# VectorE does the first shared job right behind the slots and the block lists in pieces; TensorE's waits ahead of the blocks stand at their first use

## The chip, the cores and the metric

One core of one Trainium2 chip runs the whole program. The metric is the device time of one execution in microseconds (us). A span is the same execution as the profiler sees it, from the first to the last instruction. The engines are TensorE (PE), VectorE (DVE), ScalarE (ACT), GpSimd (POOL) and SyncE (SP, which here issues the loads and stores).

## The reference, cut to what matters

The program is a transformer layer on x of 2 x 1024 tokens by 256 values: an attention with a bias and a mask, a second attention, then a mixture of experts and a block that is applied to the best three quarters of the tokens. The change lies in the mixture of experts:

```
logits = (x @ wt.T + logits_g) / 2 ; scores = softmax(logits)   # 8 experts
topk_w, topk_idx = top_k(scores, 2) ; topk_w normalized
y_all[e] = (leaky(x @ w_gate[e]) * (x @ w_up[e])) @ w_down[e]   # e = 0..7
y = sum over the 2 chosen experts of topk_w * y_all
p = leaky(x @ sw_gate) * (x @ sw_up) @ sw_down                  # the shared expert, 256 wide
y = y + p
scores = y @ w_router ; top_idx = top_k(scores, 768 of 1024)
out = y, but gelu(y @ w_block) at top_idx
```

## The kernel before, in words

The tokens lie in 16 tiles of 128, in four chunks of 512 (NC_ = 4). Both the shared expert and the eight routed experts are computed in full float32.

**Routing.** VectorE computes the top two experts of each token and gives each of the 4096 (token, expert) pairs a row, a slot, of the array XS in device memory, so that the pairs of one expert lie together, padded to blocks of 128 rows. There are NBK = 39 blocks. The slots are in SI; its write (L2727) raises s_route to SLOT_IDS.

**Scatter in.** From then on POOL scatters the token tiles into XS, 32 indirect DMAs of one tile each (L2380 for the first choice, L2389 for the second), in the order chunk 0 and 1 first choice, 0 and 1 second, 2 and 3 first, 2 and 3 second.

**Block lists.** VectorE orders the 39 blocks by which can be complete after how many token tiles: three waves with 8, 12 and 16 tiles scattered, which hold READY = 9, 17 and 39 blocks in all. table(w) writes for each block of wave w its expert (EBI) and its first row in XS (STI), some 15 tiny VectorE instructions on one partition, and raises s_route to TABLE[w]. SP reads STI[b] into a register and loads block b of XS into the ring XB of six buffers; the loads of a wave wait for TABLE[w] and for its scatters (s_first, s_second). TensorE reads EBI[b] into a register (read_experts), with which it addresses the expert's weights.

**Shared jobs.** The shared expert is cut into 8 jobs (4 chunks x 2 halves of 128 hidden values). gate_up(n) is 4 matmuls of TensorE into psG and psU, leaky_product(n) is 3 VectorE instructions on 128x512 that make HH (L2776, L2777, L2780), down(n) is 4 matmuls into psY (L2437), and after each two jobs shared_result(c) copies psY to Y (L2784). psG, psU and HH have two buffers each. gate_up(0) and gate_up(1) are issued before the slots are known. NF = 6 jobs (0 to 5) are done ahead of the blocks, two behind them. Eight column_product(n) (L2787) are put between the jobs: each writes one more column of the down weights WD, which the last matmul of a block reads.

**Blocks.** TensorE's loop over i does, in this order: turned(i) (transposes block i, L2495), wide(i-1) (gate and up matmuls of block i-1, L2505), turned_back(i-2) (L2515), narrow(i-3) (down matmul, L2523). ScalarE copies between them in the order XT(i) (L2619), HT(i-2) (L2626), YB(i-3) (L2632). VectorE makes a copy of the indices IB (L2811), the three instructions of the product of block b (L2819, L2821, L2825) and, for the first twelve blocks, one score_product (L2791). POOL scatters each block's result YB to YS (L2406). XB and YB are the two halves of the array XY, six buffers each: YB(b) for b of 6 and more waits until the whole trio (b-6)//3 of results has landed in YS.

**The order at the change.** Every engine executes its instructions in the order in which they are issued. Before the change VectorE does, behind the slots: the counts of whole blocks, table(0), the weights of the choices (R1, W2), need and cnt, then job 0. table(1) and table(2) follow jobs 2 and 4. TensorE waits for TABLE[0] ahead of down(1), reads up to 17 experts while the shared jobs run, and ahead of the first block waits for all six products, for y_done 3 (the third shared_result) and for all eight column products.

The functions and the loops, with their line numbers:

Of the kernel before, what the change touches and what calls it, by code (L numbers as in the profile page):

```python
# [22 lines left out]
E, M = 8, 128  # L23
# [65 lines left out]
def program(nc, x, bias1, cond, mask, g_in, null_bias, wq1, wkv1, wo1, g_out, wq2T, bq2, wk2T, bk2, wv2T,  # L89
            bv2, gamma, wtT, wgT, w_gate, w_up, w_down, sw_gate, sw_up, sw_down, w_router, w_block, out):  # L90
    top = ExitStack()
    with top:
# [2064 lines left out]
        with ExitStack() as s3:  # L2157
# [6 lines left out]
            with ExitStack() as st:  # L2164
# [246 lines left out]
                def _(pe):  # L2411
# [69 lines left out]
                    for n in range(NF):  # L2481
                        if n >= 1 and n + 1 < NF:
                            gate_up(n + 1)
                        if n == 1:
                            pe.wait_ge(s_route, TABLE[0])
                        read_experts(min(5 * n, READY[0]) if n < 4 else READY[1])
                        down(n)
# [40 lines left out]
                    pe.wait_ge(hh_done, NF)  # L2528
                    pe.wait_ge(y_done, NC_ - 1)
                    pe.wait_ge(s_side, SIDE_COLUMN)  # L2530
                    for i in range(NBK + 3):
                        read_experts(max(READY[1], i + 5))
                        if i < NBK:
                            turned(i)
                        if 1 <= i <= NBK:
                            wide(i - 1)
                        if 2 <= i <= NBK + 1:
                            turned_back(i - 2)
                        if i >= 3:
                            narrow(i - 3)  # L2540
# [123 lines left out]
                def _(dve):  # L2664
# [62 lines left out]
                    dve.tensor_copy(SI[:, :, :], SF[:, :, :]).then_inc(s_route, 1)  # L2727
                    for w in range(2):
                        chain(dve.tensor_tensor(CMP[0:1, :, :], early_n[:, w, :].unsqueeze(2).broadcast_to([1, E, NT]),
                                                fill_f[0:1, :].unsqueeze(1).broadcast_to([1, E, NT]), ALU.is_gt), True)  # L2730
                        chain(dve.tensor_reduce(whole[:, w, :], CMP[0:1, :, :], AX_X, ALU.add), True)
                    chain(dve.tensor_copy(whole[:, 2, :], nbk[0:1, :]))
                    chain(dve.memset(given[:, :], 0.0), True)

                    def table(w):
                        lo = READY[w - 1] if w else 0
                        m = READY[w] - lo
                        new = slice(lo, lo + m)
                        chain(dve.tensor_tensor(waiting[:, :], whole[:, w, :], given[:, :], ALU.subtract), True)
                        chain(dve.tensor_tensor(BEF[0:1, :, :], tri[0:1, :, :], waiting[:, :].unsqueeze(1).broadcast_to([1, E, E]),  # L2740
                                                ALU.mult), True)
                        chain(dve.tensor_reduce(ahead[:, :], BEF[0:1, :, :], AX_X, ALU.add), True)
                        chain(dve.tensor_tensor(shift[:, :], bof[0:1, :], ahead[:, :], ALU.subtract))
                        chain(dve.tensor_tensor(step[:, :], ahead[:, :], waiting[:, :], ALU.add), True)
                        chain(dve.tensor_tensor(shift[:, :], shift[:, :], given[:, :], ALU.add))
                        chain(dve.tensor_tensor(EBC[:, 0:m, :], step[:, :].unsqueeze(1).broadcast_to([1, m, E]),
                                                blk_f[:, 0:m].unsqueeze(2).broadcast_to([1, m, E]), ALU.is_le), True)
                        chain(dve.tensor_reduce(EBF[:, 0:m], EBC[:, 0:m, :], AX_X, ALU.add))
                        chain(dve.tensor_tensor(step[:, 0:E - 1], shift[:, 1:E], shift[:, 0:E - 1], ALU.subtract), True)
                        chain(dve.tensor_scalar(EBI[:, new], EBF[:, 0:m], float(E - 1), None, ALU.min))  # L2750
                        chain(dve.tensor_tensor(EBC[:, 0:m, 0:E - 1], EBC[:, 0:m, 0:E - 1],
                                                step[:, 0:E - 1].unsqueeze(1).broadcast_to([1, m, E - 1]), ALU.mult), True)
                        chain(dve.tensor_reduce(STF[:, 0:m], EBC[:, 0:m, 0:E - 1], AX_X, ALU.add), True)
                        chain(dve.scalar_tensor_tensor(out=STF[:, 0:m], in0=STF[:, 0:m], scalar=shift[:, 0:1], in1=blk_f[:, 0:m],
                                                       op0=ALU.add, op1=ALU.add), True)
                        dve.tensor_scalar(STI[:, new], STF[:, 0:m], float(P), None, ALU.mult).then_inc(s_route, 1)
# [6 lines left out]
                    table(0)  # L2763
                    chain(dve.scalar_tensor_tensor(out=R1[:, :], in0=top_s[:, 0, :], scalar=1e-20, in1=top_s[:, 1, :],
                                                   op0=ALU.add, op1=ALU.add), True)
                    chain(dve.reciprocal(R1[:, :], R1[:, :]), True)
                    for k in range(2):
                        chain(dve.tensor_tensor(W2[:, k, :], top_s[:, k, :], R1[:, :], ALU.mult))

                    dve.wait_ge(s_wb, 32)  # L2770
                    chain(dve.tensor_copy(need[:, :], need_i[:, :]))
                    chain(dve.memset(cnt[:, :, :], 0.0), True)

# [19 lines left out]

                    for n in range(NF + 1):
                        if n < NF:
                            leaky_product(n)
                            column_product(n)
                        if n >= NS_ and n % NS_ == 0:
                            shared_result(n // NS_ - 1)
                        if n in (2, 4):  # L2800
                            table(n // 2)
                    for n in range(NF, E):
                        column_product(n)
                    dve.wait_ge(y_done, NC_ - 1)
                    dve.wait_ge(s_side, SIDE_COLUMN)
                    for b in range(NBK + 1):
                        if 1 <= b <= NT - TT:
                            score_product(b - 1)
# [125 lines left out]
```

## Time and profile before

| | us |
|---|---|
| median of 3 runs | 380.38 (377.99 to 381.49) |
| profiled execution: its own time | 377.98 |
| profiled execution: span | 376.1 |
| TensorE busy / weight loads | 309.6 / 214.1 |
| VectorE busy | 220.5 |
| ScalarE busy | 136.1 |
| POOL busy | 151.3 |

The mean granted clock of TensorE over the span is 0.90 of full speed. The stretch of the change runs from 210.8 us, when the slots are known, over the shared jobs (218.5 to 246.4 us) and the 39 blocks (248.6 to 317.6 us); the end phase (two shared jobs, combination, second top-k, block) follows until 376.1 us. TensorE is busy over 80% of the span, but the shares are averages over stages: what a stage waits for is read from its timeline.

### The profile page before, as it was taken

To read this page: it belongs to the slowest core of one execution; us is meant where nothing else is said; L and a number is where in the kernel's file an instruction comes from. 1 tells how busy PE (TensorE), PEld (TensorE's weight loads), DVE (VectorE), ACT (ScalarE), POOL (GpSimd) and SP (SyncE) were. 2 spreads that over 40 slices of the span, in tenths; PEclk is the share of its full clock that TensorE was granted. 3 is DMA by queue.
4 is the path that set the end of the run, shared out by engine and by line. 5 is a ranking of instruction groups with operands and counts; after the bars stand their busy time and mean duration, and the time that the engine had idled before them with its cause. 6 is when DMAs were issued, how large, how long until landed. Compare 5 with 4: busy or idle time off the path is not lost. (4 is left out here: it accounts for less than half of the span.)

```text
span 376.1 us, 6114 instructions
## 1 busy us (share of the span) xinstructions
PE 309.6 (82%) x1659; PEld 214.1 (57%) x1659; DVE 220.5 (59%) x851; ACT 136.1 (36%) x428; POOL 151.3 (40%) x244
## 2 busy tenths in 40 slices
PE   7799999979988879768388179879999999864970
PEld 6366676546764644344174145458877786553850
DVE  4564445333632746366245758848655553699996
ACT  1365767552010741626021000015555554034420
POOL 1349989770030004161500377774565556000000
PEclk9999999999999975568769779989999999969895
DMA  5969920000059400000010032645555431660014
GB/s 153 292 139 323 298 93 3 2 1 2 0 179 264 105 0 0 2 0 0 7 46 1 34 107 99 182 127 147 161 160 164 127 105 44 208 240 3 2 59 164
DMA packets 36074, 38.01 MB, mean 101 GB/s; under 512 B 5182, under 2 KB 31679, under 8 KB 36034
## 3 DMA queue, kind: packets, MB, share of 16 engines
q1 hardware_dynamic: 31650, 29.04, 28.4%
q0 software_dynamic: 3408, 8.43, 6.1%
q8 instruction: 16, 0.26, 0.3%
q14 instruction: 24, 0.20, 0.2%
q10 hardware_dynamic: 976, 0.08, 0.2%
HBM read 21.88 MB, written 16.57 MB: 102 GB/s over the span
## 5 line engine op out<-in xcount | busy, mean ns | idle before, releaser
L2406 POOL DMA_INDIRECT YS<-XY,IB x39 | 38.4, 985 | 28.3 <-DVE IB L2811 17.1
L2505 PE MATMUL psU<-WGU,XT 128*128 x156 | 42.3, 395 | 0.1
L2619 ACT COPY XT<-psG 128x256 f32<-128x256 f32 x39 | 14.7, 377 | 51.0 <-PE psG L2495 50.7
L1193 POOL TENSOR_SCALAR UU<-UU,rs 128x257 f32<-128x257 f32 x32 | 29.9, 935 | 0.0
L2505 PEld LDWEIGHTS psU<-WGU,XT 128*128 128x128 f32 x156 | 27.3, 195 | 3.5 <-issue 0.7
L1360 ACT ACTIVATE UU<-UU,nm 128x129 f32<-128x129 f32 x64 | 28.4, 452 | 0.7 <-DVE nm L1469 0.7
L1469 DVE CUSTOM_DVE_ANT_0 UU<-psS,BI 128x129 f32<-128x129 f32 x64 | 19.1, 356 | 14.3 <-PE psS L1248 14.3
L2437 PE MATMUL psY<-SD,HH 128*128 128x256 f32 x64 | 16.9, 410 | 12.7 <-DVE HH L2780 12.7
L2380 POOL DMA_INDIRECT XS<-AI,SI x16 | 16.0, 1002 | 26.6 <-DVE SI L2727 22.0
L2819 DVE TENSOR_SCALAR LK<-psU 128x128 f32<-128x128 f32 x39 | 11.4, 291 | 24.3 <-PE psU L2505 24.3
L1192 POOL TENSOR_SCALAR UU<-UU,rs 128x129 f32<-128x129 f32 x32 | 19.7, 615 | 13.5 <-DVE rs L1479 13.4
L2523 PE MATMUL psY<-WD,HT 128*128 x78 | 23.5, 384 | 0.0
L2437 PEld LDWEIGHTS psY<-SD,HH 128*128 128x128 f32 x64 | 13.0, 207 | 17.5 <-issue 12.8
L870 POOL TENSOR_TENSOR AI<-X,CB 128x256 f32<-128x256 f32 x12 | 8.3, 723 | 35.5 <-DVE CB L1015 35.5
L1487 DVE COPY PT<-psTt 128x384 f32<-128x384 f32 x16 | 8.9, 556 | 20.3 <-PE psTt L1319 20.3
L707 PE MATMUL psS<-KE,QE 4*128 4x256 f32 x64 | 11.9, 501 | 8.6 <-DVE nm L929 8.6
L2626 ACT COPY HT<-psY 128x128 f32<-128x128 f32 x39 | 10.4, 267 | 23.2 <-PE psY L2515 23.2
L2389 POOL DMA_INDIRECT XS<-AI,SI x16 | 16.0, 997 | 4.8 <-issue 3.7
L2495 PE MATMUL psG<-ident,XY 128*128 128x128 f32 x78 | 15.6, 286 | 2.4 <-DVE WD L2787 2.2
L2632 ACT COPY XY<-psY 128x257 f32<-128x257 f32 x39 | 14.6, 374 | 6.8 <-PE psY L2523 6.3
L1002 DVE COPY PT<-psTt 128x512 f32<-128x512 f32 x16 | 10.9, 690 | 10.1 <-PE psTt L746 10.0
L2576 PE MATMUL psU<-WB,FT 128*128 128x256 f32 x64 | 15.4, 393 | 1.7 <-ACT X L2648 0.9
(342 smaller groups left out, 722.6 us busy)
## 6 DMA issues: line engine op xcount, KB each, us to landing
XS<-PZ SPq DMA_DIRECT2D x1, 5011.5 KB, 20.7
XY<-XS SPq DMA_DIRECT2D x39, 128.5 KB, 2.5
YR<-YS SPq DMA_DIRECT2D x2, 1028.0 KB, 6.8
BI<-in_bias SPq DMA_DIRECT2D x4, 512.0 KB, 8.8
X<-in_x SPq DMA_DIRECT2D x2, 768.0 KB, 10.1
out_dram<-X SPq DMA_DIRECT2D x3, 512.0 KB, 3.0
WGU<-YS SPq DMA_DIRECT2D x1, 1028.0 KB, 10.3
XY<-YS SPq DMA_DIRECT2D x1, 1028.0 KB, 12.4
```

What stands on the lines that cost most here:

```text
L1192: pool.tensor_scalar(U[:, he, 0:W1], U[:, he, 0:W1], rs[:, d, 2 * he:2 * he + 1], None, ALU.mult)
L1193: pool.tensor_scalar(U[:, he, W1:WU], U[:, he, W1:WU], rs[:, d, 2 * he + 1:2 * he + 2], None, ALU.mult).then_inc(n_done, 1)
L1360: act.activation(U[:, he, cols], U[:, he, cols], ACT.Exp, scale=-1.0, bias=nm[:, d, n:n + 1], accum_out=rs[:, d, n:n + 1]).then_inc(exp_do ...
L1469: dve.tensor_tensor_reduce(out=U[:, he, cols], in0=psS[2 * (d % 2) + he][:, cols], in1=BI[:, h, cols], scale=-1.0, scalar=-NEG, op0=ALU.ad ...
L2380: pool.indirect_dma_start(XS[:, :], bass.IndirectOffsetOnAxis(ap=SI[:, 0, t:t + 1], axis=0), AI[:, t, :], None).then_inc(s_first[c], 16)
L2389: pool.indirect_dma_start(XS[:, :], bass.IndirectOffsetOnAxis(ap=SI[:, 1, t:t + 1], axis=0), AI[:, t, :], None).then_inc(s_second[(0, 0, 1 ...
L2406: pool.indirect_dma_start(YS[:, :], bass.IndirectOffsetOnAxis(ap=IB[:, b, n:n + 1], axis=0), YB[i][:, n, :], None, bounds_check=2 * NTOK - ...
L2437: mm = pe.matmul(psY[c % 2][:, t, :], HH[n % 2][:, t * P:(t + 1) * P], SD[:, m, :], start=m == 0 and t % 2 == 0, stop=m == NS_ - 1, skip_g ...
L2495: mm = pe.transpose(psG[b % 2][:, (k * SUB + n) * P:(k * SUB + n + 1) * P], XB[b % RING][:, n, k * P:(k + 1) * P], ident[:, :])
L2505: mm = pe.matmul(psU[b % 2][:, n * D:(n + 1) * D], XT[b % 2][:, k, n * P:(n + 1) * P], WGU[:, k, bass.ds(which[b], 1), :].rearrange("p a m ...
L2523: mm = pe.matmul(result(b)[:, 0:D + 1], HT[b % 2][:, n * P:(n + 1) * P], WD[:, bass.ds(which[b], 1), :].rearrange("p a d -> p (a d)"), sta ...
L2576: mm = pe.matmul(psU[t % 2][:, 0:D], FT[:, k, t * P:(t + 1) * P], WB[:, k, :], start=k == 0, stop=k == KD - 1)
```

## The change

Nothing is computed in another way; instructions change place on VectorE, and three waits and the reads of experts change place on TensorE. SP, POOL and ScalarE are untouched.

- VectorE: leaky_product(0) comes right behind the slots. The counts of whole blocks and table(0), now cut into table_counts, table_experts and table_rows, follow around job 1. table(1) and table(2) are cut in the same way and put between the jobs; table_rows(2) is done inside the block loop at b = 2, and the weights of the choices with need and cnt at b = 3. The wait for s_wb stands ahead of the first column product.
- TensorE: the wait for TABLE[0] stands ahead of down(2), in place of down(1). Experts are read two at a time from n = 3 on, six before the blocks, and one in each turn of the block loop. The waits for y_done 3 and for the column products stand ahead of narrow(0) (i = 3), in place of ahead of turned(0).

```
                     for n in range(NF):
                         if n >= 1 and n + 1 < NF:
                             gate_up(n + 1)
-                        if n == 1:
+                        if n == 2:
                             pe.wait_ge(s_route, TABLE[0])
-                        read_experts(min(5 * n, READY[0]) if n < 4 else READY[1])
+                        read_experts(max(0, 2 * n - 4))
                         down(n)
...
                     pe.wait_ge(hh_done, NF)
-                    pe.wait_ge(y_done, NC_ - 1)
-                    pe.wait_ge(s_side, SIDE_COLUMN)
                     for i in range(NBK + 3):
-                        read_experts(max(READY[1], i + 5))
+                        read_experts(i + 6)
                         if i < NBK:
                             turned(i)
                         if 1 <= i <= NBK:
                             wide(i - 1)
                         if 2 <= i <= NBK + 1:
                             turned_back(i - 2)
+                        if i == 3:
+                            pe.wait_ge(y_done, NC_ - 1)
+                            pe.wait_ge(s_side, SIDE_COLUMN)
                         if i >= 3:
                             narrow(i - 3)
...
-                    for n in range(NF + 1):
-                        if n < NF:
-                            leaky_product(n)
-                            column_product(n)
-                        if n >= NS_ and n % NS_ == 0:
-                            shared_result(n // NS_ - 1)
-                        if n in (2, 4):
-                            table(n // 2)
-                    for n in range(NF, E):
-                        column_product(n)
+                    leaky_product(0)
+                    whole_blocks()
+                    table_counts(0)
+                    leaky_product(1)
+                    table_experts(0)
+                    table_rows(0)
+                    dve.wait_ge(s_wb, 32)
+                    column_product(0)
+                    column_product(1)
+                    leaky_product(2)
+                    column_product(2)
+                    shared_result(0)
+                    table_counts(1)
+                    leaky_product(3)
+                    column_product(3)
+                    table_experts(1)
+                    table_rows(1)
+                    leaky_product(4)
+                    column_product(4)
+                    shared_result(1)
+                    table_counts(2)
+                    leaky_product(5)
+                    column_product(5)
+                    table_experts(2)
+                    column_product(6)
+                    column_product(7)
+                    shared_result(2)
                     dve.wait_ge(y_done, NC_ - 1)
                     dve.wait_ge(s_side, SIDE_COLUMN)
                     for b in range(NBK + 1):
+                        if b == 2:
+                            table_rows(2)
+                        if b == 3:
+                            choice_weights()
                         if 1 <= b <= NT - TT:
                             score_product(b - 1)
```

whole_blocks holds the six instructions at L2729 to L2733, table_counts those at L2739 to L2745, table_experts L2746 to L2750, table_rows L2751 to L2761. At the ends of table_counts and table_experts a wait for the engine's own last result is added; choice_weights holds L2764 to L2772.

## Rows read from the trace of the kernel before

**Rows 1.** Chain that ended last (start, length, what), first and last block.

```profile
247.97 0.34 DVE X L2787
...
248.57 0.91 PE psG L2495 x4
...
319.50 2.06 DMA YS<-XY,IB
```

**Rows 2.** Timeline of VectorE, slots to job 0 (start, length, line, operation).

```profile
210.75 0.27 DVE L2729 TENSOR_TENSOR CMP<-early_n,fill_f 1x128 f32<-1x128 f32 x1
...
213.24 0.21 DVE L2746 TENSOR_TENSOR EBC<-step,blk_f 1x72 f32<-1x72 f32 x1
...
215.28 0.18 DVE L2764 SCALAR_TENSOR_TENSOR R<-top_s 128x16 f32<-128x16 f32 x1
...
216.22 0.69 DVE L2776 TENSOR_SCALAR SA<-psG 128x512 f32<-128x512 f32 x1
```

**Rows 3.** Timeline of TensorE, the shared jobs ahead of the blocks.

```profile
218.51 3.43 PE L2437 MATMUL psY<-SD,HH 128*128 128x256 f32 x8 [10.35 <-DVE HH L2780]
...
240.69 1.89 PE L2437 MATMUL psY<-SD,HH 128*128 128x256 f32 x8
244.37 1.99 PE L2437 MATMUL psY<-SD,HH 128*128 128x256 f32 x8 [1.80 <-DVE HH L2780]
```

**Rows 4.** Timeline of VectorE, table(2), job 5 and the third shared result.

```profile
240.30 0.32 DVE L2746 TENSOR_TENSOR EBC<-step,blk_f 1x176 f32<-1x176 f32 x1
...
241.17 0.30 DVE L2751 TENSOR_TENSOR EBC<-EBC,step 1x154 f32<-1x154 f32 x1
...
242.20 0.67 DVE L2776 TENSOR_SCALAR SA<-psG 128x512 f32<-128x512 f32 x1
...
246.41 1.23 DVE L2784 COPY Y<-psY 128x1024 f32<-128x1024 f32 x1 [1.75 <-PE psY L2437]
```

**Rows 5.** Timeline of POOL, last scatter into XS and first scatters of results.

```profile
252.62 1.20 POOL L2389 DMA_INDIRECT XS<-AI,SI  x1 [0.30 <-issue]
256.49 1.00 POOL L2406 DMA_INDIRECT YS<-XY,IB  x1 [2.67 <-DVE IB L2811]
257.80 1.00 POOL L2406 DMA_INDIRECT YS<-XY,IB  x1 [0.30 <-issue]
```

**Rows 6.** Landing of the scatters at L2389, then of the loads at L2339.

```profile
DMA to landing us min/median/max: 2.6/3.1/3.5
...
DMA to landing us min/median/max: 2.2/2.5/4.6
```

**Rows 7.** Timeline of SP: the loads of the blocks begin.

```profile
235.32 26.43 SPq L2339 DMA_DIRECT2D XY<-XS  x14
```

**Rows 8.** Chain that ended last: wide(10), wide(12) and wide(34).

```profile
266.52 0.87 PE psU L2505 x4
...
269.82 0.97 PE psU L2505 x4
...
307.88 0.87 PE psU L2505 x4
```

**Rows 9.** Timeline of ScalarE: YB(6), then XT(10).

```profile
264.71 0.37 ACT L2632 COPY XY<-psY 128x257 f32<-128x257 f32 x1 [0.17 <-PE psY L2523]
264.98 0.38 ACT L2619 COPY XT<-psG 128x256 f32<-128x256 f32 x1
```

**Rows 10.** Timeline of VectorE: the product of block 4 begins.

```profile
257.65 0.29 DVE L2819 TENSOR_SCALAR LK<-psU 128x128 f32<-128x128 f32 x1 [0.28 <-PE psU L2505]
```

**Rows 11.** Windows: us, busy PE, PEld, DVE, ACT, POOL, clock, DMA, GB/s.

```profile
208.20:218.50 10.30, 0.00 (x0) 0.02 (x1) 9.28 (x42) 0.00 (x0) 5.16 (x6) 0.65 0.14 51
...
246.40:248.60 2.20, 0.03 (x1) 0.06 (x2) 2.10 (x7) 0.00 (x0) 1.61 (x3) 1.00 0.23 80
...
249.60:251.70 2.10, 2.10 (x6) 1.62 (x7) 0.00 (x0) 0.29 (x1) 1.49 (x3) 0.50 0.44 134
```

**Rows 12.** Windows of TensorE alone: us, busy, granted clock, DMA share, GB/s.

```profile
144.00:146.00 2.00, 2.00 (x12) 0.50 0.00 0
```

More of the change, by code:

```diff
@@ L2727, in _, with whole_blocks, size, table_counts @@
                     dve.tensor_copy(SI[:, :, :], SF[:, :, :]).then_inc(s_route, 1)
[L2728 to L2738, printed above, removed]
+                    def whole_blocks():
+                        for w in range(2):
+                            chain(dve.tensor_tensor(CMP[0:1, :, :], early_n[:, w, :].unsqueeze(2).broadcast_to([1, E, NT]),
+                                                    fill_f[0:1, :].unsqueeze(1).broadcast_to([1, E, NT]), ALU.is_gt), True)
+                            chain(dve.tensor_reduce(whole[:, w, :], CMP[0:1, :, :], AX_X, ALU.add), True)
+                        chain(dve.tensor_copy(whole[:, 2, :], nbk[0:1, :]))
+                        chain(dve.memset(given[:, :], 0.0), True)
+                    def size(w):
+                        return READY[w] - (READY[w - 1] if w else 0)
+                    def table_counts(w):
                         chain(dve.tensor_tensor(waiting[:, :], whole[:, w, :], given[:, :], ALU.subtract), True)
@@ L2744, in table, with table_experts @@
                         chain(dve.tensor_tensor(step[:, :], ahead[:, :], waiting[:, :], ALU.add), True)
-                        chain(dve.tensor_tensor(shift[:, :], shift[:, :], given[:, :], ALU.add))
+                        chain(dve.tensor_tensor(shift[:, :], shift[:, :], given[:, :], ALU.add), True)
+                    def table_experts(w):
+                        m = size(w)
                         chain(dve.tensor_tensor(EBC[:, 0:m, :], step[:, :].unsqueeze(1).broadcast_to([1, m, E]),
@@ L2749, in table, with table_rows @@
                         chain(dve.tensor_tensor(step[:, 0:E - 1], shift[:, 1:E], shift[:, 0:E - 1], ALU.subtract), True)
-                        chain(dve.tensor_scalar(EBI[:, new], EBF[:, 0:m], float(E - 1), None, ALU.min))
+                        chain(dve.tensor_scalar(EBI[:, READY[w] - m:READY[w]], EBF[:, 0:m], float(E - 1), None, ALU.min), True)
+                    def table_rows(w):
+                        m = size(w)
                         chain(dve.tensor_tensor(EBC[:, 0:m, 0:E - 1], EBC[:, 0:m, 0:E - 1],
@@ L2755, in table @@
                                                        op0=ALU.add, op1=ALU.add), True)
-                        dve.tensor_scalar(STI[:, new], STF[:, 0:m], float(P), None, ALU.mult).then_inc(s_route, 1)
+                        dve.tensor_scalar(STI[:, READY[w] - m:READY[w]], STF[:, 0:m], float(P), None, ALU.mult).then_inc(s_route, 1)
                         if w < 2:
@@ L2761, in table, with choice_weights @@
                             chain(dve.tensor_tensor(given[:, :], given[:, :], ahead[:, :], ALU.add), True)
[L2763 to L2772, printed above, removed]
+                    def choice_weights():
+                        chain(dve.scalar_tensor_tensor(out=R1[:, :], in0=top_s[:, 0, :], scalar=1e-20, in1=top_s[:, 1, :],
+                                                       op0=ALU.add, op1=ALU.add), True)
+                        chain(dve.reciprocal(R1[:, :], R1[:, :]), True)
+                        for k in range(2):
+                            chain(dve.tensor_tensor(W2[:, k, :], top_s[:, k, :], R1[:, :], ALU.mult))
+                        chain(dve.tensor_copy(need[:, :], need_i[:, :]))
+                        chain(dve.memset(cnt[:, :, :], 0.0), True)
                     def leaky_product(n):
```

## The prediction, made before the changed kernel ran

> **What bounds the kernel now.** I read the chain of waits first. Its last unbroken part begins at 247.97 us with a column product of VectorE, which releases the first transposes of TensorE at 248.57; from there it is TensorE's work of the 39 blocks, and behind the last block a scatter, a load and VectorE's combination [rows 1]. So the time is set by when the blocks begin, by how fast they follow each other, and by a tail that the change does not touch. The next view is TensorE's timeline ahead of the blocks: it is idle for 10.35 us, until down(0) at 218.51, and its release is VectorE's HH [rows 3]. VectorE's timeline says why. The slots are out and its next instruction starts at 210.75; then come block counts and list (to 215.28) and the weights of the choices (to 216.22), and only then job 0, whose matmuls had long been issued [rows 2]. From 218.51 to 240.85 (gate_up(5) ends 0.16 after down(4) is let in at 240.69, an overlap as modelled) TensorE works without a gap, so in that stretch it is the bound [rows 3]. At the end it is VectorE again: job 5 starts at 242.20, behind table(2) (240.30 and on), and holds down(5) until 244.37 [rows 3, 4]. The third shared result (246.41, 1.23 us) and two column products then hold the first block [rows 1, 4].
>
> **What the change does, step by step.**
>
> Job 0 first. From the start of its first instruction to down(0) it takes 218.51 - 216.22 = 2.29 us [rows 2, 3]. Started at 210.75, down(0) starts at 213.04, 5.5 us earlier. The slots themselves are not moved, so POOL's scatters start and end as before. The clock does not come into it twice: down(0) took 3.43 us against 1.89 for down(4), half speed behind the idle stretch, whose mean granted clock was 0.65 [rows 3, 11]. I leave it so after the idle of 5 us.
>
> The lists in pieces. Between job 0 and job 2 VectorE has counts (210.75 to 213.24, 2.5 us), job 1 (2.1), the experts and rows (213.24 to 215.28, 2.0) and two column products (0.34 each [rows 1]): from 212.8 this ends at 220.1. Two added waits for its own results cost some 0.1 each. gate_up(2) ends at 213.0 + 3.4 + 3.4 = 219.9, so VectorE is late by 0.3 us, and that is hidden, since down(2) stands behind gate_up(3) in TensorE's queue. After this, each pair of jobs gives VectorE 2 x 2.1 of products, 2 x 0.34, one shared result of 1.14 (246.41 to the column product that follows) and one list of 3.1 at most, 9.1 us against the 10.3 us of TensorE for two gate_ups and two downs (3.43 and 1.7 each). So TensorE stays the bound and gate_up(5) ends at 213.04 + 22.34 = 235.4, with 22.34 = 240.85 - 218.51 [rows 3]. The wait for TABLE[0] ahead of down(2) costs nothing: the list is there at 219.0, down(2) comes at 225. It is also the wait behind which down(1) does not queue any more.
>
> Job 5. Its list is cut: table_counts(2) fits ahead, the rest comes behind. The product starts at 235.4 rather than 242.20, another 1.4 us, and down(5) runs from 237.5 to 239.2. Sum so far 5.5 + 1.4 = 6.9 us.
>
> The waits. turned(0) needs block 0 in XB: SP's loads start at 235.32 and take 2.5 us (2.2 to 4.6) [rows 6, 7], so 237.8, up to 239.9. It starts at about 239.2, against 248.57: 9.3 us earlier. This is the place to be careful, since VectorE is not there yet. After job 5 (237.45) it has a column product (0.34), table_experts(2) (0.87), two column products (0.68), and the shared result from 239.4 to 240.5. Then the copy of indices, one score product (0.4) and the product of block 0, three instructions of 0.29, until 242.1. Block 1 queues behind table_rows(2), 242.20 - 241.17 = 1.03 us, block 2 behind the weights of the choices, 216.22 - 215.28 = 0.94 [rows 2, 4]. With these, the products of blocks 1 and 2 end at 244.6 and 246.9, TensorE waits for both, and wide(5) starts at about 249.4. Before, it was at 266.52 - 5 x 1.65 = 258.3, with 1.65 from wide(10) to wide(12) [rows 8]. VectorE, which in steady state waits 0.28 us per block [rows 10], has caught up. So blocks stand 8.9 us earlier here. The two late jobs cost 2.0 us of a possible 10.9.
>
> The reads of experts. wide(12) to wide(34), in whose turns a read stands, is 38.06 / 22 = 1.73 us per block against 1.65 [rows 8], so 0.08 per read, called 0.1. Twelve turns get a read that they had not, one loses it. Five of them lie between wide(5) and wide(10), which is then wanted at 249.4 + 5 x 1.73 = 258.1.
>
> **What is late next: the ring of results.** POOL is in order. Its last scatter into XS starts at 252.62 whatever VectorE does; that is 1.20 + 0.30 us, and the first result can start at 254.1, in place of 256.49, where it was waiting. At a pitch of 1.31 the third result starts at 256.7 [rows 5]. YB(6) needs all three landed. The trace shows no landing for these; the scatters into XS, of the same size and engine and beside the same loads, took 3.1 us (2.6 to 3.5) [rows 6], and the last scatter of all, with nothing beside it, 2.06 [rows 1]. I take 3.1, the row of the same conditions: 259.85. ScalarE, which wanted YB(6) at about 256.5, copies it then, and XT(10) stands behind it in its queue, 0.27 after the start of YB(6) and 0.38 long [rows 9]. wide(10) therefore starts at about 260.7, not at 258.1: a stall of 2.6 us on TensorE. Before, it was 266.52. The gain is 5.8 us; two further reads and one that goes take 0.1. Later trios are safe: POOL needs 1.31 per block, TensorE 1.65 to 1.73. Sum 5.7, rounded down to 5.6.
>
> The ends of this term. Landing at 2.06 gives 6.7, at 3.5 gives 5.2. Where POOL's start behind its waits costs more than 0.30 (up to the 2.67 - 1.2 that it idled before; 1 us taken as the end), 4.2. The data of the second wave (block 9) are the last scatters but five, so near 247, plus 3.5 and 2.5 to 4.6: 253 to 255; needed at 254.7 and covered by the stall. The rule of the Trainium skill, page "DMA: Bandwidth & Descriptors", section on the anatomy of one DMA (2.0 us plus the bytes by 436 GB/s) would give an estimate of 2.3 us for a 128 KB scatter and a gain of 6.5; the scatter rows of this trace are above it, and I keep them.
>
> The tail, 317.6 us on, moves as a whole: its waits are for the blocks, not for anything absolute. So a span of 370.5, and a time of 377.98 - 5.6 = 372.4 for the profiled execution. That one was the fastest of those shown; against the median of 380.38 it is **374.8**.
>
> **The rivals.**
>
> B, the clock. TensorE stalls 2.6 us at wide(10). Behind an idle of 2.2 us (and one of 1.80 shortly before) its clock was at half, the 1.2 GHz level, from 249.6 to 251.7 at least. The price is what down(0) paid, 3.43 us for matmuls that take 1.7 at full clock [rows 3, 11]. If it falls here: gain 3.9, 376.5. Against it: in the idle stretch of 10.30 us the mean of 0.65 means that full clock was granted for 3.1 us of idleness, more than 2.6, and there is unbroken work ahead of this stall. The page "TensorE: Matmul & The Clock Gate" of the Trainium skill, section on the clock gate, says that half rate is the default, which activity lifts and idleness restores; the trace agrees in kind. Earlier drops, in 239 to 249, are covered by the ring.
>
> C, small gains. The ring with the slow ends (4.2) and the clock together (1.7) leave 2.5 us, 377.9, which is no difference by the bound below. For it: several queues now overlap that did not. Against: each end is the far one.
>
> D, slower. The clock falls at the stall and does not come back while the blocks run: at 144 us TensorE was busy 2.00 of 2.00 us at 0.50 [rows 12]. A block whose work is all TensorE's then takes 1.65 us more. It decides from 11 us of low clock on (5.6 / 0.5); 16 us cost 8.0, and the time is 382.8. Against: behind the idle of 10.35 us only down(0) was slow [rows 3].
>
> **Chances.** Forecast 0.60, B 0.22, C 0.11, D 0.07. About 1% (3.8 us) is what a measurement of this kernel can tell from no change. Faster by more: the forecast and half of B (its 3.9 lies on the bound), 0.71, called 0.72. Within: the other half of B and C, 0.22. Slower 0.06. The range: at the low end the gain of 6.7 from the lowest run of 377.99, so 371.3; at the high end B with the 1.1 us by which the highest run lies above the median, 377.6, and a part of C. 371.5 to 378.0.
>
> **What would show it.** Right: down(0) near 213.0; down(5) ending near 239.2; turned(0) without a wait for VectorE; idle TensorE of about 1 us each at blocks 1 and 2; one stall at wide(10) with ScalarE's YB(6) waiting for a DMA; POOL's first result at 254.1 with no idle before it; no stall behind block 10. Wrong: no wait at YB(6) (then the gain is nearer 8), gaps at turned(9) (loads are the bound), a clock of 0.5 behind 260, or gaps ahead of the gate_ups (VectorE is the bound of the jobs).

## The result, and the profile after

| | before | after |
|---|---|---|
| median, us | 380.38 (17 runs, 374.07 to 382.73) | 373.16 (17 runs, 369.9 to 376.65) |
| ratio | | 0.9852, 95% interval 0.9819 to 0.9885 |
| profiled execution: own time / span | 377.98 / 376.1 | 373.7 / 371.9 |
| slots known (start of the write of SI) | 210.66 | 213.00 |
| from there to the end of the span | 165.44 | 158.90 |

The ratio compares only the runs of each kernel within 1.5% of its fastest, the medians are of all its runs. By the ratio the change makes the kernel faster by 5.6 us (4.4 to 6.9; 0.0148 of 380.38), and 5.6 was predicted. That the two agree to the tenth is chance: the two medians differ by 7.2 us, and the two traces, as counted below, by 6.5. The median of 373.16 lies in the range of 371.5 to 378.0.

The two spans differ by 4.2 us only. The reading of the traces begins with why: the slots come 2.34 us later in the execution after, and nothing ahead of them was changed. Over all traces of this case they come between 208.75 (e9) and 214.24 (e5). So the stretch that the change can act on is measured from the slots, and there the gain is 165.44 - 158.90 = **6.5 us**. All times called "behind the slots" are counted so. What the scatter of the earlier part does to the timed ratio stays inside its interval.

The chain of waits that ended last, answering to [rows 1] (start, length, what):

```profile
241.10 1.99 PE psY L2437 x8
243.09 0.23 PE psG L2495 x2
...
245.68 0.29 DVE HH L2852
245.97 0.22 DVE EBC L2759
...
247.98 0.30 DVE HH L2852
...
262.04 0.37 ACT XT L2620
...
262.54 1.13 PE psU L2505 x4
...
315.54 2.06 DMA YS<-XY,IB
```

It now goes from down(5) into the first block without VectorE in between. From 245.03 to 248.33 it then runs over VectorE, which it did not before: the product of block 0, table_rows(2) (EBC and on), the product of block 1. Further on it has a new step, ScalarE's XT ahead of a block. The last scatter starts 102.54 behind the slots, 6.3 us earlier than before.

TensorE after, answering to [rows 3]: start, duration, line, operation, shapes, and the idle time before with its releaser.

```profile
215.37 3.75 PE L2437 MATMUL psY<-SD,HH 128*128 128x256 f32 x8 [4.87 <-DVE HH L2786]
218.92 2.67 PE L2426 MATMUL psG<-FT,SG 128*128 128x512 f32 x4
221.43 1.88 PE L2426 MATMUL psU<-FT,SU 128*128 128x512 f32 x4
...
238.62 1.89 PE L2437 MATMUL psY<-SD,HH 128*128 128x256 f32 x8
241.10 1.99 PE L2437 MATMUL psY<-SD,HH 128*128 128x256 f32 x8 [0.58 <-DVE HH L2786]
242.93 0.60 PE L2495 MATMUL psG<-ident,XY 128*128 128x128 f32 x4
```

down(0) comes 2.37 us behind the slots, in place of 7.85; its idle time is 4.87 in place of 10.35. It is still slow (3.75), and so is the first half of the gate_up behind it (2.67, where the next takes 1.88). down(5) waits 0.58 in place of 1.80, and the first transposes stand directly behind it: the 2.21 us for VectorE's WD are gone.

VectorE after, answering to [rows 2, 4]:

```profile
213.00 0.18 DVE L2728 CAST SI<-SF 128x32 int32<-128x32 f32 x1
213.09 0.68 DVE L2782 TENSOR_SCALAR SA<-psG 128x512 f32<-128x512 f32 x1
...
238.90 0.69 DVE L2782 TENSOR_SCALAR SA<-psG 128x512 f32<-128x512 f32 x1 [0.54 <-PE psU L2426]
...
243.13 1.23 DVE L2790 COPY Y<-psY 128x1024 f32<-128x1024 f32 x1
...
245.88 0.30 DVE L2759 TENSOR_TENSOR EBC<-EBC,step 1x154 f32<-1x154 f32 x1
...
248.19 0.17 DVE L2772 SCALAR_TENSOR_TENSOR R<-top_s 128x16 f32<-128x16 f32 x1
```

Job 0 follows the slots, job 5 waits for its matmuls and for nothing of VectorE's own, and the late pieces stand between the products of blocks 0, 1 and 2.

TensorE in the first blocks, where VectorE and the reads of experts are late. ("issue" names no releaser; ahead of 246.77 TensorE's queue is at the read of L2479, a load of EBI and register work, from 246.01 to 246.61.)

```profile
246.77 0.41 PE L2495 MATMUL psG<-ident,XY 128*128 128x128 f32 x2 [0.42 <-issue]
...
248.33 0.33 PE L2515 MATMUL psY<-ident,HH 128*128 128x128 f32 x1 [0.20 <-DVE HH L2852]
...
251.52 0.41 PE L2495 MATMUL psG<-ident,XY 128*128 128x128 f32 x2 [0.24 <-issue]
```

Then the ring of results. POOL first, answering to [rows 5], and ScalarE and TensorE, answering to [rows 8, 9]:

```profile
254.60 0.96 POOL L2389 DMA_INDIRECT XS<-AI,SI  x1 [0.30 <-DVE IB L2838]
255.87 1.00 POOL L2406 DMA_INDIRECT YS<-XY,IB  x1 [0.30 <-ACT XY L2633]
257.17 1.00 POOL L2406 DMA_INDIRECT YS<-XY,IB  x1 [0.30 <-issue]
258.47 0.98 POOL L2406 DMA_INDIRECT YS<-XY,IB  x1 [0.30 <-issue]
```

```profile
261.76 0.37 ACT L2633 COPY XY<-psY 128x257 f32<-128x257 f32 x1 [1.64 <-DMA YS<-XY,IB]
262.03 0.38 ACT L2620 COPY XT<-psG 128x256 f32<-128x256 f32 x1
```

```profile
260.30 1.03 PE L2505 MATMUL psU<-WGU,XT 128*128 x4
262.54 1.13 PE L2505 MATMUL psU<-WGU,XT 128*128 x4 [0.42 <-ACT XT L2620]
```

POOL goes from its last scatter into XS to the results with no idle but the usual 0.30. The third result starts at 258.47; ScalarE's YB(6) is let go by its landing at 261.76, 3.3 us later; XT(10) stands behind it, and wide(10) behind that, 2.24 us after wide(9) in place of the usual 1.7. This wait did not exist before.

The granted clock (windows: stretch, length, busy time of PE, PEld, DVE, ACT, POOL, clock, DMA share, GB/s), answering to [rows 11]:

```profile
213.20:216.00 2.80, 0.63 (x2) 0.57 (x3) 2.66 (x6) 0.00 (x0) 1.54 (x2) 0.59 0.04 13
216.00:220.00 4.00, 4.00 (x10) 2.86 (x9) 3.63 (x14) 0.00 (x0) 3.09 (x4) 0.50 0.35 120
220.00:240.00 20.00, 20.00 (x62) 11.59 (x62) 16.61 (x57) 0.00 (x0) 15.21 (x18) 0.99 0.33 107
...
262.00:315.00 53.00, 51.90 (x268) 40.51 (x267) 28.05 (x120) 28.43 (x93) 32.44 (x34) 1.00 0.46 131
```

Half speed (the 1.2 GHz level) up to about 220.5, since the granted clock is 0.75 in 220 to 221; full speed afterwards, across the wait at wide(10) and all blocks behind it.

One table for all executions whose signals came in time (what that means stands under "late signals" below), in us behind the slots ("product of block 38" is its last instruction):

```
                      before  after   e6      e11     e12
down(0)                 7.85   2.37    2.38    2.37    2.37
  its duration          3.43   3.75    3.75    1.97    3.75
job 5 starts           31.54  25.90   25.79   23.72   27.36
down(5)                33.71  28.10   27.98   25.92   29.53
turned(0)              37.91  29.93   29.82   27.75   35.17
wide(5)                47.55  40.47   40.29   37.89   45.07
wide(10)               55.70  49.54   48.99   46.45   53.22
product of block 38   105.07  98.76   97.91   95.92  101.95
end                   165.44 158.90  157.92  156.73  162.01
```

### The profile page after: what moved, and what is told of

Read it like the earlier page. It is cut to its first block and busy times, and to the rows that moved or that the text cites. A ratio compares the mean times of both kernels' runs of the same rounds, so it can differ in the third digit from the quotient of the medians.

```text
span 371.9 us, 6118 instructions
## 1 busy us (share of the span) xinstructions
PE 313.3 (84%) x1659; PEld 213.6 (57%) x1659; DVE 221.0 (59%) x851; ACT 135.9 (37%) x428; POOL 150.7 (41%) x244
## 5 line engine op out<-in xcount | busy, mean ns | idle before, releaser
L1487 DVE COPY PT<-psTt 128x384 f32<-128x384 f32 x16 | 8.9, 556 | 20.3 <-PE psTt L1319 20.3
L2577 PE MATMUL psU<-WB,FT 128*128 128x256 f32 x64 | 17.0, 423 | 1.7 <-ACT X L2649 0.9
L2389 POOL DMA_INDIRECT XS<-AI,SI x16 | 15.7, 982 | 4.8 <-issue 3.4
## 6 DMA issues: line engine op xcount, KB each, us to landing
XS<-PZ SPq DMA_DIRECT2D x1, 5011.5 KB, 20.7
WGU<-YS SPq DMA_DIRECT2D x1, 1028.0 KB, 10.2
```

The source lines that it names most:

```text
L2577: mm = pe.matmul(psU[t % 2][:, 0:D], FT[:, k, t * P:(t + 1) * P], WB[:, k, :], start=k == 0, stop=k == KD - 1)
```

## The experiments

**Two halves and a quarter of the change** (e1, e2, e3), and the change with the reads of experts ahead of the blocks (e4). e1 is the kernel after with TensorE's part undone, e2 the kernel before with TensorE's part done. e1's edit:

```diff
-                        if n == 2:
+                        if n == 1:
                             pe.wait_ge(s_route, TABLE[0])
-                        read_experts(max(0, 2 * n - 4))
+                        read_experts(min(5 * n, READY[0]) if n < 4 else READY[1])
...
                     pe.wait_ge(hh_done, NF)
+                    pe.wait_ge(y_done, NC_ - 1)
+                    pe.wait_ge(s_side, SIDE_COLUMN)
                     for i in range(NBK + 3):
-                        read_experts(i + 6)
+                        read_experts(max(READY[1], i + 5))
...
-                        if i == 3:
-                            pe.wait_ge(y_done, NC_ - 1)
-                            pe.wait_ge(s_side, SIDE_COLUMN)
```

e3 is the kernel before with one move, to right behind the write of SI (the definition of leaky_product moves with it):

```diff
+                    leaky_product(0)
...
                         if n < NF:
-                            leaky_product(n)
+                            if n:
+                                leaky_product(n)
```

e4 is the kernel after with the reads taken early:

```diff
-                        read_experts(max(0, 2 * n - 4))
+                        read_experts((0, 0, 5, READY[0], READY[1], READY[1])[n])
...
-                        read_experts(i + 6)
+                        read_experts(max(READY[1], i + 5))
```

> VectorE's new order alone; TensorE's waits and reads as before the change. Counted from the slots (start of the write of SI) to the end of the span, where the kernel before has 165.4 us and the changed one 158.9. Theory (the ring of results is what ends the stretch): the blocks start behind the third shared result, 1.7 us later than in the changed kernel, but wide(10) was held by the landing of the first trio in the changed kernel, so at most 0.8 of it is left at block 10, and 0.3 comes back from the reads: 159.4 to 159.7. Rival (the start of the blocks passes through in full): 160.6.

> TensorE's moved waits and reads alone; VectorE's order as before. Theory: job 0 stays late, down(5) stays at 33.7 us behind the slots; the first turned comes at 35.5 instead of 37.9, block 0's product 2.6 earlier, twelve more reads in the loop take about 0.9 back, no stall at the ring (first trio landed at 49, wanted at 51.4): 163.6, a gain of 1.8. Rival (the waits were covered by VectorE anyway, the reads cost): 165.4 to 166.3.

> The kernel before with one edit: job 0's three instructions right behind the slots, the lists whole and in their old places. Theory: down(0) 5.5 us earlier, but VectorE becomes the bound of the later jobs (list 2 stands ahead of job 5, which starts at 27.6 behind the slots), down(5) at 29.7 against 33.7 before and 28.1 in the changed kernel; all of the 4.0 us reach the end since the ring has 5 us to spare at that point: 161.4. Rival (the gain is that of the whole idle time, 5.5): 159.9.

> The changed kernel, but 17 experts are read during the shared jobs as before the change (one turn later), so that the first twelve turns of the block loop have no read. Theory (ring): wide(10) is released by the landing of the first trio and stays at 49.5 us behind the slots; only the reads of two later turns are saved: 158.7. Rival (the reads are on the path): 12 reads of 0.1 and the idle 0.7 us at the first turns: 157.0 to 157.7.

Measured, against 405.85 for the kernel before on the same chip in turns:

```
e1 vector alone   397.80   ratio 0.9827 (0.9752 to 0.9903)
e2 tensor alone   401.36   ratio 0.9878 (0.9798 to 0.9958)
e3 job 0 first    403.19   ratio 0.9936 (0.9903 to 0.9970)
e4 early reads    397.97   ratio 0.9845 (0.9769 to 0.9920)
```

No expectation in numbers applies: the kernel before itself took 25 us more than in the first comparison, and the traces show why. The same happened again in the repeats e5 and e7 (the edit of e1), e8 (of e3) and e9 (of e2), so this is told once here. Three executions of e1's kernel (e1, e5, e7) were profiled; VectorE in e7:

```profile
234.40 0.69 DVE L2781 TENSOR_SCALAR SA<-psG 128x512 f32<-128x512 f32 x1 [5.38 <-remote]
...
259.01 0.69 DVE L2781 TENSOR_SCALAR SA<-psG 128x512 f32<-128x512 f32 x1 [20.08 <-remote]
```

and TensorE in e7, which should have let it go:

```profile
231.71 1.88 PE L2426 MATMUL psG<-FT,SG 128*128 128x512 f32 x4
233.43 1.88 PE L2426 MATMUL psU<-FT,SU 128*128 128x512 f32 x4
...
261.21 3.48 PE L2437 MATMUL psY<-SD,HH 128*128 128x256 f32 x8 [19.19 <-DVE HH L2785]
```

gate_up(4) ends at 235.3 and job 4 begins at 259.0. I call this **late signals** (the last section shows that they are not TensorE's alone): the matmuls are recorded as done, and the semaphore that says so rises over 20 us later (in e5 the rise for gate_up(4), due at 236.8, is recorded at 260.64 with the next one at 260.83). Job 4 starts 46.3 to 46.5 us behind the slots in every such trace of e1 to e5 and e7 to e9, whatever the order of the work (44.2 in e10); after the change, with the signals in time, it is 20.7. The kernel before pays for it too, by its times (401 to 409 us). What of the change can still be read there is what comes behind job 4.

> VectorE's new order alone, once more, to see where VectorE's pauses of 4 and 20 us (its matmuls long done, jobs 3 and 4) belong. If they belong to the kernel's order, they are here again and the rest behind the slots is 185.7 us; if to the chip of that call, they are gone, and the values of the first theory hold: 159.4 to 159.7 by the ring, 160.6 by the rival.

> VectorE's new order alone, on a chip where jobs 3 and 4 are not let go late (if it is such a one). Theory (the ring hides what the blocks' start loses): first turned 1.7 us later than in the changed kernel, at 31.6 us behind the slots, but the rest behind the slots 159.4 to 159.7 against 158.9. Rival (the start of the blocks passes through in full): 160.6.

> The kernel before with job 0 right behind the slots and nothing else changed. Theory (VectorE's whole lists bound the later jobs): down(5) at 29.7 us behind the slots against 33.7 before and 28.1 in the changed kernel, and 4.0 us of gain reach the end: the rest behind the slots is 161.4 against 165.4. Rival (all of the idle time, 5.5): 159.9.

> TensorE's moved waits and reads alone. Theory: first turned at 35.5 us behind the slots against 37.9, twelve reads of 0.1 take some back, no stall at the ring: the rest is 163.6 against 165.4. Rival (VectorE covers the waits, the reads cost): 165.4 to 166.3.

e5 is one run, 400.04 beside one of before of 402.5. The others against 404.82: e7 398.42, ratio 0.9873 (0.9804 to 0.9942); e8 404.62, ratio 0.9992 (0.9950 to 1.0034); e9 397.97, ratio 0.9870 (0.9812 to 0.9929). All had late signals again (before, there: 401 to 409 us), e7 to e9 on a chip on which e6 and a run of before did not. e5 asked whether the pauses belong to the order of the kernel or to the chip; by its trace and by these times they belong to neither alone. In us behind the slots, with TensorE's clock low at down(5) unless said ("block 5" is the last instruction of its product):

```
                        job 4   job 5   down(5)  turned(0)  block 5   end
e3 job 0 first          46.47   52.92   55.09    61.08      74.6    191.1
e8 job 0 first          46.35   52.80   54.97    60.96      74.6    191.3
e2 tensor alone         46.33   52.77   54.95    58.46      71.3    188.4
e9 tensor alone         46.31   52.76   54.94    58.51      70.1    186.0
e1 vector alone         46.44   51.10   53.29    58.44      70.2    185.7
e5 vector alone         46.50   51.16   53.35    56.71      68.5    184.0   (down(5) at full clock, 1.99)
e7 vector alone         46.43   51.09   53.28    56.64      68.5    184.0   (down(5) at full clock, 1.99)
e4 both, reads early    46.40   51.06   53.25    56.83      68.8    184.4
```

Four readings. The cut of list 2 takes job 5 from 6.45 to 4.66 behind job 4, so 1.8 us; where the signals are in time, job 5 goes from 27.36 (e12) to 25.90, so 1.5, and 1.4 was predicted. TensorE's moved waits take the start of the blocks from 6.0 to 3.6 behind down(5) in the old order of VectorE (e3 to e9), so 2.4 us, and from 5.15 to 3.58 in the new (e1 to e4, the reads taken early), so 1.6. At the end the sizes are larger: against e8, e9 is 5.2 us earlier and e1 5.6, e4 with both 6.8. A part of this is TensorE's clock, which is 0.56 in e8 over 270 to 280 (58.7 to 68.7 behind its slots) and 1.00 in e9 over 270 to 280 (61.3 to 71.3 behind its slots); so the gains here are not those of a kernel whose signals are in time. Both parts shorten the same queue of VectorE, so their gains do not add. Job 0 first alone gives little or nothing (0.9936, with an interval that ends below 1, and 0.9992, with one that holds 1), since there is a wait of 20 us behind it that swallows 5.5. This is the rival of a hidden gain, made real: it depends on what comes next, not on the move itself. And e4's question, what the reads in the block loop cost: from the product of block 0 to that of block 5 it takes 8.97 us in e4, with no read in these turns, and 9.61 after the change, so up to 0.6 us, between an execution with late signals and one without. No run of the whole change was made under late signals; e4, and e10 with three edits more, come nearest.

**Does the ring of results hold wide(10)?** e6 gives YB nine buffers in place of six, with a third semaphore for the third trio (for which two other semaphores are made one; the lines shown leave this out):

```diff
+RY = 9
...
-                XY = tensor(st, "XY", [P, 2 * RING, D + 1])
+                XY = tensor(st, "XY", [P, RING + RY, D + 1])
...
-                            if b >= RING:
-                                act.wait_ge(s_ys[trio(b)], whole_trio(b - RING))
+                            if b >= RY:
+                                act.wait_ge(s_ys[trio(b)], whole_trio(b - RY))
```

> The changed kernel with nine buffers for the blocks' results in place of six, so that YB(6) waits for nothing and YB(9) for the first trio. Where the chip delivers TensorE's semaphores at once: theory (ring): wide(10) starts about 0.6 us earlier, at 48.9 us behind the slots, and the rest behind the slots is 158.3; rival (nothing waited at the ring): 158.9. Where jobs 3 and 4 are let go late, as in the first five runs (job 4 at 46.4 behind the slots), the results come when POOL is long free, and ring 6 and ring 9 are the same by both.

One run, 369.45, beside one of before of 378.7, signals in time. ScalarE and TensorE of e6:

```profile
256.94 0.37 ACT L2633 COPY XY<-psY 128x257 f32<-128x257 f32 x1 [0.17 <-PE psY L2523]
257.21 0.38 ACT L2620 COPY XT<-psG 128x256 f32<-128x256 f32 x1
```

```profile
256.96 1.11 PE L2505 MATMUL psU<-WGU,XT 128*128 x4
...
258.67 1.09 PE L2505 MATMUL psU<-WGU,XT 128*128 x4
```

The wait of YB(6) for a DMA is gone, wide(10) follows wide(9) by 1.71 us with no idle, 48.99 behind the slots against 49.54, and the end comes at 157.92, 0.98 earlier, where the theory had 158.3 and the rival 158.9. So the ring was what held wide(10), and it cost 0.4 us there (9.07 from wide(5) to wide(10), against 8.70 here). Of the 0.98 at the end, 0.18 was there at wide(5), ahead of the ring, so up to 0.8 is the ring's. The difference of the ends is from one execution of each.

**The clock, the ring and the late weights together.** e10 and e11 are one kernel: e6, and 11 matmuls without a use that TensorE does while it would idle ahead of down(0), and the weights of the choices at b = 14 in place of 3.

```diff
+                    for _ in range(11):
+                        pe.matmul(psY[1][:, 0, :], ident[:, :], FT[:, 0, 0:D], start=True, stop=True)
                     pe.wait_ge(s_route, SLOTTED)
...
-                        if b == 3:
+                        if b == 14:
                             choice_weights()
```

> The changed kernel with three edits: nine buffers for the results; eleven matmuls of 256 columns (their results are not used) in TensorE's idle stretch between the slots' counts and down(0), which should hold the clock; and the weights of the choices at b = 14 in place of b = 3. Theory (clock at down(0) and gate_up(2), VectorE's late job and the ring are each a term that is left): down(0) 1.7 us long instead of 3.75, down(5) at 26.1 instead of 28.1 where VectorE becomes the bound of the jobs, 0.9 less at block 2: the rest behind the slots is 155.1 against 158.9 (157.9 with nine buffers alone). Rival (the early stretch is covered by VectorE in any case, so the clock there is worth nothing): 157.0 to 157.9.

> The three edits of e10 again (nine buffers for results, eleven matmuls of 256 columns in the idle stretch ahead of down(0), the choices' weights at b = 14), for a call in which TensorE's signals arrive in time. From e10 the start is known: down(0) 1.96 us long, job 3 at 14.5 us behind the slots. Theory: job 5 starts at 24.0, down(5) at 26.2, first turned at 28.1, the rest behind the slots 155.1, and a ratio of 0.975 to the kernel before. Rival (VectorE covers the early stretch, POOL's pitch of 1.3 us for results or the loads of the second wave hold blocks 9 to 15 instead): 157.0 to 157.9, ratio 0.980. If the signals are late again (job 4 at 44 to 46 behind the slots) it repeats e10: about 0.98.

e10 had late signals: 397.95, ratio to before 0.9789 (0.9679 to 0.9899). e11 had them in time: **371.79 against 381.48, ratio 0.9763 (0.9714 to 0.9812)**. It is below both kernels; against the change itself it was not timed side by side, and its ratio to before is 0.0089 lower. TensorE of e11:

```profile
211.02 5.00 PE L2472 MATMUL psY<-FT,ident 128*128 128x256 f32 x22
216.04 1.97 PE L2437 MATMUL psY<-SD,HH 128*128 128x256 f32 x8
...
239.59 1.99 PE L2437 MATMUL psY<-SD,HH 128*128 128x256 f32 x8 [0.94 <-DVE HH L2788]
...
242.29 0.44 PE L2497 MATMUL psG<-ident,XY 128*128 128x128 f32 x2 [0.49 <-DMA XY<-XS]
...
245.39 0.41 PE L2497 MATMUL psG<-ident,XY 128*128 128x128 f32 x2 [0.34 <-DMA XY<-XS]
```

and its clock:

```profile
211.00:216.00 5.00, 5.00 (x24) 4.10 (x23) 4.49 (x13) 0.00 (x0) 1.16 (x1) 1.00 0.01 3
216.00:218.00 2.00, 1.98 (x10) 1.78 (x10) 1.72 (x9) 0.00 (x0) 1.40 (x3) 1.00 0.27 95
```

With TensorE busy in the 4.9 us, the granted clock stays at 1.00, down(0) takes 1.97 in place of 3.75, and down(1) comes 7.61 behind the slots in place of 10.15: half speed behind the idle cost the change 2.5 us in that stretch. Against e6, 2.1 of it are left at job 5 and at turned(0), 2.4 at wide(5), where the late weights have their part, 2.0 at block 38 and 1.2 at the end. What is late next are SP's loads of the blocks, which this kernel does not start earlier (24.5 behind the slots, 24.6 after the change): TensorE waits 0.49 and 0.34 for them. The theory of e11 held for the shared jobs (job 5 at 23.72, 24.0 predicted; turned(0) at 27.75, 28.1 predicted) and failed behind them: the end of 156.73 lies nearer to the 157.0 of the rival than to the 155.1 of the theory. Of what was gained at block 38, 0.8 is gone at the end, in a tail that nothing was changed in; the cause of that is open. The filler matmuls and the late weights were not tried singly.

**Job 0 first, with the signals in time.** e12 is e3's kernel again.

> Job 0 right behind the slots alone, again, for a call in which TensorE's signals arrive in time. Theory (VectorE's whole lists bound the later jobs): down(5) at 29.7 us behind the slots (33.7 before, 28.1 changed), rest 161.4 against 165.4, ratio 0.989. Rival (all of the idle time): 159.9, ratio 0.985. If the signals are late again: no gain, as in e3 and e8 (0.9936, 0.9992).

375.09 against 381.48, ratio 0.9809 (0.9747 to 0.9871); behind the slots 162.01, where the theory had 161.4 and the rival 159.9. VectorE and TensorE of e12:

```profile
236.63 0.32 DVE L2755 TENSOR_TENSOR EBC<-step,blk_f 1x176 f32<-1x176 f32 x1
...
238.65 0.67 DVE L2730 TENSOR_SCALAR SA<-psG 128x512 f32<-128x512 f32 x1
```

```profile
240.82 3.43 PE L2437 MATMUL psY<-SD,HH 128*128 128x256 f32 x8 [1.90 <-DVE HH L2734]
...
246.46 0.63 PE L2495 MATMUL psG<-ident,XY 128*128 128x128 f32 x4 [2.21 <-DVE WD L2788]
```

down(0) is as early as in the whole change, but job 5 stands behind list 2, TensorE idles 1.90 and its clock is low behind that (down(5) 3.43 in place of 1.99), and the blocks wait 2.21 for WD as they did before. So by the traces job 0 first is worth 165.44 - 162.01 = 3.4 us, and the lists in pieces with the moved waits the other 3.1. The timed ratio of e12 would say that job 0 first is worth more (0.0191 of 381.48, 7.3 us, more than the whole change by its own ratio); its interval leaves out the theory's 0.989 and holds the rival's 0.985. Traces behind the slots and timed medians disagree here by about as much as the slots themselves scatter from execution to execution; a split of the 6.5 finer than a microsecond is not to be had from single traces.

## Why the prediction was right, point by point

Times are behind the slots, predicted (the text's absolute times less 210.66) and measured.

- **Job 0 first, down(0) 5.5 earlier.** 5.48. Right.
- **The clock behind the shorter idle, "I leave it so".** This term was mis-sized: the prediction put nothing for a difference. down(0) took 3.75 in place of the 3.43 of before, and the half speed reached into gate_up(2) (2.67 in place of 1.88), for 1.1 us together: job 5 was let go at 25.90 in place of 24.74. Before, the clock came back within down(0), some 3 us behind its start (0.50 in 220 to 221, 0.76 in 221 to 222); after, some 5 us behind its start (0.75 in 220 to 221). The shorter idle did not bring it back earlier. e11 shows that the whole half-speed stretch could be had back.
- **VectorE keeps up between the jobs.** Right: no gap on TensorE from down(0) to gate_up(5). Job 5 no longer stands behind a list.
- **Lists and waits at the start of the blocks.** turned(0) without a wait for VectorE, as forecast, at 29.93 in place of 28.54; of the 1.4 us between them 1.2 come from the clock above. The idle times at blocks 1 and 2 are 0.42, 0.20 and 0.24 in place of two of 1 us each, but the stretch as a whole was sized well: from turned(0) to wide(5) it takes 10.54, and 10.2 was predicted. wide(5) stands at 40.47 in place of 38.74, 1.7 late; 1.4 of this is what turned(0) brought along.
- **The ring of results.** The place, the chain and the releaser were right: POOL's third result at 45.47 (predicted 46.0), YB(6) let go at 48.76 (49.2), wide(10) at 49.54 (50.0). The landing took 3.3, where 3.1 was taken from the scatters of the same conditions. POOL's last scatter into XS took 0.96 in place of the 1.20 of before, which is some of the 0.5 that the ring came earlier. The estimate of 2.3 us from the Trainium skill, page "DMA: Bandwidth & Descriptors", section on the anatomy of one DMA, would have let it go a microsecond sooner; the trace disagrees with it here, where loads ran beside the scatter, while the last scatter of all, with nothing beside it, took 2.06.
- **The stall of 2.6 us** was only 0.4. It is the difference of two times, and the one that came from VectorE and TensorE was 1.7 us later than computed. This is why the total was right although the terms ahead were not: wide(10) is the later of two chains, the ring's was sized well, and what the other chain lost on its way was taken out of the wait. It was luck that this chain lost 1.7 and not more than the 2.6 that the wait could take up; what it lost beyond that would have been lost at wide(10) as well. The gain at wide(10) was 6.2 us, 5.8 predicted.
- **Later trios safe, tail as a whole.** 6.3 at block 38 and 6.5 at the end, and no wait for a load at turned(9). Right; the last 0.2 is within what two executions of the same work differ.
- **Rivals B and D, the clock at the stall.** Not seen: 1.00 over 262 to 315. The stall was too short to put it to the test as it was posed. The rule of the Trainium skill, page "TensorE: Matmul & The Clock Gate", section on the clock gate, that idleness brings half speed and activity lifts it, agrees with down(0) here and with e11.
- **Rival C, small gains.** One of its ends, POOL later than 0.30 behind its last scatter, was excluded by the row at 255.87.

## What to carry to other kernels

Where two chains meet in one wait, size the one that will be later after the change with the most care; an error in the other is absorbed, and the same absorption means that a further improvement of it buys little. When an idle stretch of TensorE is shortened but not removed, charge the slow clock in full to the first matmuls behind it and to those after them; busying TensorE with matmuls nobody needs was worth 2.5 us there, and together with the weights of the choices moved 1.2 us at the end, in one execution of each. And compare single traces from the last point that the change cannot have touched, not from their start.

## What the runs showed of the hardware that was not expected

**Late signals.** The kernel before took 374 to 384 us in some sets of runs and 401 to 409 in others, both on one chip (378.7 and 404.82), and the kernels with edits likewise. In the long ones TensorE's matmuls of jobs 3 and 4 are recorded in time, and VectorE begins job 4 20.3 (e9) to 26.5 us (e4) behind the end of its matmuls: 46.3 to 46.5 us behind the slots in e1 to e5 and e7 to e9, 44.2 in e10. In the time between, POOL does its 32 scatters; the last one starts at 41.3 to 42.0 us behind the slots in all traces, late or not:

```profile
253.87 0.96 POOL L2389 DMA_INDIRECT XS<-AI,SI  x1 [0.30 <-issue]
```

(e7; 41.29 behind its slots.)

It is not TensorE's signals alone. SyncE's own register work for the loads of the blocks (L2338) is slow in the same stretch, first after the change (237 to 252), then in e7 (236 to 258), as the length of one instruction in ns, shortest/median/longest:

```profile
L2338 SPq FUSED_REGOPS  x9: 152/152/164, 237.1 to 247.8; - x9
```

```profile
L2338 SPq FUSED_REGOPS  x3: 164/700/700, 236.5 to 251.1; - x3
```

So in e7 SyncE issues the first three loads of blocks 27.3, 35.7 and 44.1 us behind the slots, and the next from 46.3 on at 1.1 us each, as after the change (24.6, 25.7, 26.9 and on); from 46.3 on its instructions are as short as there, and at 46.4 job 4 begins. The traces of the two kinds differ in one more thing: from 5 to 45 us behind the slots they hold 733 to 856 records of a semaphore's rise where the signals are in time, and 103 to 153 where they are late, although POOL issues the same scatters. Whether rises came late, or records were lost, and whether the recording of the execution has itself a part in the delay, no run shows. That the end of the scatters frees the signals is a guess from the order in time. Nothing was tried that moves the scatters' end, so the cause is open, and so is why one set of runs shows it and another does not.

**What was not tried:** TensorE's part alone, VectorE's part alone and the early reads with the signals in time; so the split of the 3.1 us between lists, waits and reads rests on the late executions (at the start of the blocks 1.8 for the list, 1.6 to 2.4 for the waits, not additive).
